# The last stage of a fused mixer and mixture-of-experts kernel: x1 held in SBUF, added by VectorE and GpSimd, and stored with plain DMAs

## The chip, the cores and the metric

The kernel runs on one core of a Trainium2 chip. The metric is the device time of one execution in microseconds, and lower is better. The kernel before has a median of 1121.13 us in three runs (1115.91 to 1122.24).

## The reference

x has the shape (4, 1024, 256), that is 4096 tokens of 256 values. Two residual blocks follow one another:

```python
x = x + _layernorm(_L0_attn_ref(_layernorm(x), ...))   # linear, conv, scan (cumprod, cumsum), gates
x = x + _layernorm(_L0_ffn_ref(_layernorm(x), ...))    # router, 8 experts with top 2, shared expert
```

The first line is called the mixer here, and its result is **x1**. In the second line each token goes to two of eight experts of 1024 hidden units (`silu(clip(gate)) * up @ down`) and to a shared expert of 256; the weighted sum of these is called **acc**. The output is `x1 + layernorm(acc)`, where the layer norm subtracts the mean of a token's 256 values and divides by the root of their variance plus 1e-5.

## The kernel before, in words

All tensors are fp32. Wherever a product must be exact, a value is split into a high part and a low part of type fp32r, and three matmuls stand for one.

**Mixer (to about 450 us).** Four batches of 1024 tokens are worked through in halves of 512, in an order that is written out by hand for every engine. x1 goes to the DRAM scratch `x1_scratch` (`store_x1`, L389, eight stores of 512 KB), the normalized tokens are scattered by expert to `xs_scratch` (L1232), and the shared expert's result goes to `acc_scratch`.

**Experts (about 450 to 1070 us).** `experts()` runs 39 slots. A slot is 256 tokens of one expert (8 steps), or 128 for the seven small slots n = 4, 8, ..., 28, whose weights have a ring of their own (`single_ring`, in the places of `xnt`, `w_sh`, `n2` and of `h`, `s`, `g`). On TensorE, slot follows slot without a gap. SyncE's queue (SP) loads weights and rows in `turn`; it waits there for TensorE (`down_done`) before it overwrites a chunk. `slots` unrolls the first slots, then runs a loop of four slots per pass, then unrolls slots 29 to 38. GpSimd adds each slot's result to `acc_scratch` with indirect accumulating DMAs (L1409). Beside this, SP moves x1 in `move_x1`, one chunk after each of the turns 2 to 8: the 4096 tokens are NC = 8 chunks of 512 tokens, four tiles of 128 x 256 each. The even chunks are copied from `x1_scratch` straight to the output in DRAM (L1376), the odd chunks are loaded to SBUF in the place of `e_both` (L1378).

**Last stage (from about 1070 us to the end).** After the last accumulating DMA, SP issues eight loads of acc (L1392, 512 KB each). Then four engines work on a chunk c in turn:

- VectorE, `moments_of(c)`: four `bn_stats` (L1673), four `bn_aggr` (L1678) and two small `tensor_scalar` (L1681, L1682). It signals `moments`.
- GpSimd, `root(c)`: a power of 128 x 4 (L1419) and a product (L1421). It signals `rs_ready`.
- ScalarE: four activations of 128 x 256 (L1590). They signal `normed`.
- The residual: for an odd chunk VectorE adds x1 in SBUF (`add_x1`, L1688, 128 x 1024) and SP stores the sum to the output (L1396); for an even chunk GpSimd issues an accumulating DMA (`add_out`, L1427) that adds acc to the x1 that already lies in the output.

Each engine goes through a fixed list. VectorE: moments 0 to 3, add 1, moments 4 and 5, add 3, moments 6 and 7, adds 5 and 7. GpSimd: roots 0 to 2, accumulating DMA 0, roots 3 and 4, DMA 2, roots 5 and 6, DMA 4, root 7, DMA 6. The program ends when SP has seen all stores of both kinds land (L1397, L1398).

Of the kernel before, what the change touches and what calls it, by code (L numbers as in the profile page):

```python
# [67 lines left out]
def mixer(nc, x, w_e, w_s, weights, full, consts, shared, xs_dram, x1_dram, acc_dram, fill, vec, ident,  # L68
# [3 lines left out]
    with ExitStack() as ctx:  # L72
# [124 lines left out]
        def free(engine, what):  # L197
# [36 lines left out]
        acc += [by_tile(flat(s[:, :, :]))]  # L234
        e_flat = e_both[:, :, :, :].rearrange("p h s c -> p (h s c)")
        x1 = [by_tile(e_flat[:, k * TC * D:(k + 1) * TC * D]) for k in range(4)]
        homes = (ring, low_d, [v[:, :, 0:W_ROW] for v in single_ring], quad(u_flat[:, R_AT:R_AT + 2 * GT * ROW]), quad(x_home[0]), quad(x_home[1]),
                 u_flat[:, R_AT + 2 * GT * ROW:R_AT + 2 * GT * ROW + DC * G].rearrange("p (c g) -> p c g", g=G),
                 cv_flat[:, 0:4 * G].rearrange("p (i g) -> p i g", g=G),
# [1012 lines left out]
TC = 4  # L1252
# [8 lines left out]
def experts(nc, ctx, w_s, xs_dram, acc_dram, x1_dram, out, group_expert, group_change, group_row, group_code, vec, ident, neg_half,  # L1261
# [24 lines left out]
    acc_loaded = [sem(f"f_loaded{c}") for c in range(NC)]  # L1286
    order, aggregated, moments = sem("f_order"), sem("f_aggregated"), sem("f_moments")
    rooted, rs_ready, normed = sem("f_rooted"), sem("f_rs_ready"), sem("f_normed")
    x1_moved, out_added = sem("x1_moved"), sem("out_added")
    sum_ready, sum_stored = sem("sum_ready"), sem("sum_stored")  # L1290

    gu_ps, down_ps = banks[0:2], [banks[2:4], banks[4:6]]
# [22 lines left out]
    def sync(sp):  # L1315
        def next_rows(i, n):
            to = (n + 1) % 2
            rows_of_slot, tiles = (P, 1) if single(n + 1) else (G, GT)
            row = sp.value_load(group_row[0:1, bass.ds(table_at(i, n + 1), 1)], min_val=0, max_val=SPARE)
            sp.wait_ge(x_turned, before(i, n, one) * DC + DC)  # L1320
            sp.wait_ge(meta_ready, before(i, n, one))
            sp.dma_start(rows[:, to, 0:tiles, :], xs_dram[bass.ds(row, rows_of_slot), :].rearrange("(t p) d -> p t d", p=P)
                         ).then_inc(rows_loaded[to], 16)

        def load_chunk(f, e, **cond):
            if f == FC - 2:
                sp.dma_start(low_d.bitcast(F32), w_s[e, f, :, 0:2 * D], **cond).then_inc(loaded[f], 16)
                sp.dma_start(ring[f][:, GU_HI:W_ROW].bitcast(F32), w_s[e, f, :, GU_HI:W_ROW], **cond).then_inc(loaded[f], 16)
                return
            sp.dma_start(ring[f].bitcast(F32), w_s[e, f, :, :], **cond).then_inc(loaded[f], 16)  # L1330

        def load_singles(part, e, wanted):
            first = sum(v.shape[1] for v in w_single[0:part])
            to = w_single[part].bitcast(F32)
            sp.dma_start(to, w_s[e, first:first + to.shape[1], :, :].rearrange("f p c -> p f c"), cond=wanted).then_inc(single_loaded, 16)

        def turn(i, n):
            if single(n):
                if n + 1 < SLOTS:
                    next_rows(i, n)  # L1340
                return
            e = sp.value_load(group_expert[0:1, bass.ds(table_at(i, n), 1)], min_val=0, max_val=E - 1)
            new = sp.value_load(group_change[0:1, bass.ds(table_at(i, n), 1)], min_val=0, max_val=1)
            last = n - 2 if single(n - 1) else n - 1
            to_come = NP + before(i, n, ones_at)
            loads_single = n % BODY in (2, 3) and single(n + BODY - n % BODY)
            for f in range(FC):
                sp.wait_ge(down_done, before(i, last, steps_at) + f + 1 + FC)
                if f == FC - 2 and single(n - 1):
                    next_rows(i, n)  # L1350
                load_chunk(f, e, cond=new)
                if f == 0 and not single(n - 1):
                    next_rows(i, n)
                if loads_single and f == 0:
                    e_single = sp.value_load(group_expert[0:1, bass.ds(to_come, 1)], min_val=0, max_val=E - 1)
                    flag = to_come + (0 if n % BODY == 2 else NS)
                    wanted = sp.value_load(group_change[0:1, bass.ds(flag, 1)], min_val=0, max_val=1)
                    if n > BODY:
                        sp.wait_ge(down_done, before(i, n - n % BODY, steps_at) + FC // 2 + FC)
                if loads_single and f < len(w_single):  # L1360
                    load_singles(f, e_single, wanted)

        def first_rows(b, par=0):
            row = sp.value_load(star[0:1, 1 + par:2 + par], min_val=0, max_val=SPARE)
            sp.dma_start(rows[:, par, :, :], xs_dram[bass.ds(row, G), :].rearrange("(t p) d -> p t d", p=P)
                         ).then_inc(rows_loaded[par], 16)

        def first_weights():
            e = sp.value_load(star[0:1, 0:1], min_val=0, max_val=E - 1)
            for f in range(FC):  # L1370
                load_chunk(f, e)

        def others():
            def move_x1(c):
                if c % 2 == 0:
                    sp.dma_start(token_rows(out)[c, :, :, :], token_rows(x1_dram)[c, :, :, :]).then_inc(x1_moved, 16)  # L1376
                else:
                    sp.dma_start(x1[c // 2], token_rows(x1_dram)[c, :, :, :]).then_inc(x1_moved, 16)  # L1378

            free(sp, "x1")  # L1380
            move_x1(0)
            free(sp, "tables")
            for c in range(1, NC):
                turn(0, c + 1)
                move_x1(c)
            slots(sp, turn, NC + 1)
            for par in range(2):
                sp.wait_ge(rows_loaded[par], 16 * before(0, SLOTS, same_at[par]))
            for par in range(2):
                sp.wait_ge(y_added[par], 16 * before(0, SLOTS, adds_at[par]))  # L1390
            for c in range(NC):
                sp.dma_start(acc[c], acc_dram[c * TC * P:(c + 1) * TC * P, :].rearrange("(t p) d -> p t d", p=P)  # L1392
                             ).then_inc(acc_loaded[c], 16)
            for c in range(1, NC, 2):
                sp.wait_ge(sum_ready, c // 2 + 1)
                sp.dma_start(token_rows(out)[c, :, :, :], acc[c]).then_inc(sum_stored, 16)  # L1396
            sp.wait_ge(sum_stored, 16 * (NC // 2))  # L1397
            sp.wait_ge(out_added, 16 * (NC // 2))  # L1398
        return first_rows, first_weights, lambda: next_rows(0, 1), others

    def gpsimd(pool):
# [11 lines left out]
        def rest():  # L1413
            free(pool, "acc")
            slots(pool, add_y)

            def root(c):
                pool.wait_ge(moments, c + 1)
                nc.gpsimd.tensor_tensor(rs[:, c, :], ve[:, c, :], neg_half[:, 0:TC], ALU.pow).then_inc(rooted, 1)  # L1419
                pool.wait_ge(rooted, c + 1)  # L1420
                nc.gpsimd.tensor_tensor(nm[:, c, :], mv[:, c, :, 0], rs[:, c, :], ALU.mult).then_inc(rs_ready, 1)  # L1421

            def add_out(c):
                if c == 0:
                    pool.wait_ge(x1_moved, 16 * NC)
                pool.wait_ge(normed, c + 1)
                nc.gpsimd.dma_start(token_rows(out)[c, :, :, :], acc[c], accum_op=ALU.add).then_inc(out_added, 16)  # L1427

            root(0)
            root(1)  # L1430
            for c in range(2, NC):
                root(c)
                if c % 2 == 0:
                    add_out(c - 2)
            add_out(NC - 2)
        return rest

    def tensor(pe):
# [103 lines left out]
    def scalar(act):  # L1542
# [39 lines left out]
        def rest():  # L1582
# [4 lines left out]
            for c in range(NC):  # L1587
                act.wait_ge(rs_ready, c + 1)
                for t in range(TC):
                    i = nc.scalar.activation(acc[c][:, t, :], acc[c][:, t, :], ACT.Identity, bias=nm[:, c, t:t + 1],  # L1590
                                             scale=rs[:, c, t:t + 1])
                i.then_inc(normed, 1)
        return first_hi, rest

    def vector(dve):
# [68 lines left out]
        def rest(plan_singles):  # L1664
# [5 lines left out]
            def moments_of(c):  # L1670
# [2 lines left out]
                    i = nc.vector.bn_stats(st[:, c, t, :], acc[c][:, t, :])  # L1673
                i.then_inc(order, 1)
                dve.wait_ge(order, c + 1)
                dve.sem_inc(seen, 1)
                for t in range(TC):
                    i = nc.vector.bn_aggr(mv[:, c, t, :], st[:, c, t, :])  # L1678
                i.then_inc(aggregated, 1)
# [2 lines left out]
                nc.vector.tensor_scalar(ve[:, c, :], mv[:, c, :, 1], 1.0, EPS, ALU.mult, ALU.add).then_inc(moments, 1)  # L1682

            def add_x1(c):
                if c == 1:
                    dve.wait_ge(x1_moved, 16 * NC)
                dve.wait_ge(normed, c + 1)
                nc.vector.tensor_tensor(acc[c], acc[c], x1[c // 2], ALU.add).then_inc(sum_ready, 1)  # L1688

            for c in range(NC):  # L1690
                moments_of(c)
                if c % 2 == 1 and c > 1:
                    add_x1(c - 2)
# [107 lines left out]
```

## Time and profile before

| | |
|---|---|
| median of three runs | 1121.13 us (1115.91 to 1122.24) |
| the profiled execution, its own time | 1116.39 us |
| its span | 1114.5 us |
| TensorE busy | 1022.9 us (92%) |
| VectorE, ScalarE, GpSimd busy | 801.9, 623.8, 286.8 us |
| mean granted TensorE clock | 0.978 |
| last expert result's DMA issued; first acc load issued | 1072.96 us; 1076.82 us |
| last instruction that computes ends; last store issued | 1105.7 us; 1105.73 us |
| DMA traffic | 210.30 MB, mean 189 GB/s |

Times inside the profile are microseconds from the start of the span. An instruction's row gives its start and its duration, and in brackets how long its engine was idle before it and what ended that. "To landing" is the time from the issue of a DMA to its completion. The profiled execution is at the low end of the three runs, 4.7 us below their median.

### The profile page before, as it was taken

How to read it: one execution, taken by the hardware profiler on the slowest of the kernel's cores; microseconds unless marked ns; L12 is line 12 of the kernel's file. 1: busy time of each engine (PE TensorE's matmuls, PEld its weight loads, DVE VectorE, ACT ScalarE, POOL GpSimd, SP SyncE). 2: the span in 40 equal slices, each digit the busy share in tenths (PEclk: the TensorE clock that was granted, in tenths of full speed). 3: DMA queues.
4: the chain of work that ended last, by engine and by line, in shares of the span. 5: the costliest groups of instructions: out<-in, count | busy, mean ns of one | idle time of the engine just before them, and what ended most of it. 6: DMA issues, size and time to landing. Idle time of an engine off the chain costs nothing.

```text
span 1114.5 us, 21512 instructions
## 1 busy us (share of the span) xinstructions
PE 1022.9 (92%) x7026; PEld 902.9 (81%) x7026; DVE 801.9 (72%) x2059; ACT 623.8 (56%) x1265; POOL 286.8 (26%) x303
## 2 busy tenths in 40 slices
PE   4889999989998999899999999999999999999930
PEld 2666677667676566799999999999999999999930
DVE  4997799888888857766666666666666666666645
ACT  6867868786876446344454444444544445445425
POOL 1133123453262273212121121211211212122134
PEclk9899999999999999999999999999999999999975
DMA  8656667886576588955563521735366822655149
GB/s 302 219 198 207 221 222 228 272 263 219 165 263 213 182 274 305 379 198 174 151 218 74 216 36 21 266 107 178 66 229 225 288 35 36 213 181 159 25 120 200
DMA packets 116518, 210.30 MB, mean 189 GB/s; under 512 B 9952, under 2 KB 75232, under 8 KB 116448
## 3 DMA queue, kind: packets, MB, share of 16 engines
q1 hardware_dynamic: 101040, 189.51, 49.0%
q0 software_dynamic: 15408, 19.93, 10.5%
q8 instruction: 35, 0.57, 0.2%
q14 instruction: 35, 0.29, 0.1%
HBM read 341.43 MB, written 86.02 MB: 384 GB/s over the span
## 4 chain that ended last, share of the span: by engine, by line
PE 75%; DVE 11%; DMA 4%; issue 3%; POOL 3%; ACT 2%; SPq 0%; DVEq 0%; ACTq 0%; POOLq 0%
PE bank L488 12%; PE bank L1461 10%; PE bank L1463 10%; PE bank L1462 10%; PE bank L1506 5%; PE bank L1508 5%; PE bank L1507 5%; PE bank L482 4%; PE bank L483 3%; PE bank L484 3%; POOL xs_scratch L1232 2%; DMA w_both<-w_split 1%; DVE h L925 1%; PE bank L1447 1%; PE bank L1479 1%
## 5 line engine op out<-in xcount | busy, mean ns | idle before, releaser
L1409 POOL DMA_INDIRECT acc_scratch<-cv,ids x71 | 111.5, 1571 | 504.1 <-DVE cv L1606 494.4
L1643 DVE TENSOR_SCALAR cv<-bank 128x256 f32<-128x256 f32 x284 | 120.5, 424 | 155.1 <-PE bank L1463 136.3
L1573 ACT ACTIVATE cv<-cv 128x256 f32<-128x256 f32 x284 | 118.4, 417 | 183.7 <-DVE cv L1643 183.7
L1461 PE MATMUL bank<-h_hi,w_both 128*128 128x256 f32 x640 | 178.0, 278 | 2.2 <-DMA w_both<-w_split 1.0
L1463 PE MATMUL bank<-h_hi,w_both 128*128 128x256 f32 x640 | 177.2, 277 | 0.0
L1462 PE MATMUL bank<-h_hi,w_both 128*128 128x256 f32 x640 | 177.2, 277 | 0.0
L1559 ACT ACTIVATE h_lo<-cv 128x256 fp32r<-128x256 f32 x256 | 106.8, 417 | 92.1 <-DVE cv L1646 92.1
L1646 DVE TENSOR_TENSOR cv<-bank,cv 128x256 f32<-128x256 f32 x284 | 120.3, 424 | 41.7 <-ACT cv L1573 34.6
L1461 PEld LDWEIGHTS bank<-h_hi,w_both 128*128 128x128 f32 x640 | 120.2, 188 | 3.1 <-issue 2.3
L1463 PEld LDWEIGHTS bank<-h_hi,w_both 128*128 128x128 f32 x640 | 120.3, 188 | 0.0
L1462 PEld LDWEIGHTS bank<-h_hi,w_both 128*128 128x128 f32 x640 | 120.3, 188 | 0.0
L482 PE MATMUL bank<-xs_hi,w_both 128*128 128x512 f32 x224 | 97.5, 435 | 20.7 <-DVE delta L875 9.7
L1624 DVE TENSOR_TENSOR w_both<-cv,h_lo 128x256 fp32r<-128x256 f32 x256 | 106.3, 415 | 0.5 <-ACT h_lo L1559 0.5
L484 PE MATMUL bank<-xs_hi,w_both 128*128 128x512 f32 x224 | 88.4, 395 | 0.0
L1508 PE MATMUL bank<-w_both 128*128 128x256 f32 x320 | 88.4, 276 | 0.0
L1506 PE MATMUL bank<-w_both,h_lo 128*128 128x256 f32 x320 | 88.4, 276 | 0.0
L1507 PE MATMUL bank<-w_both,h_lo 128*128 128x256 f32 x320 | 88.4, 276 | 0.0
L483 PE MATMUL bank<-xs_lo,w_both 128*128 128x512 f32 x224 | 88.1, 393 | 0.0
L1232 POOL DMA_INDIRECT xs_scratch<-n,slot_now x64 | 68.6, 1073 | 61.5 <-DVE slot_now L1013 32.5
L1215 POOL TENSOR_TENSOR h_lo<-h,h_hi 128x512 fp32r<-128x512 f32 x32 | 48.7, 1525 | 111.9 <-ACT h_hi L746 111.8
L482 PEld LDWEIGHTS bank<-xs_hi,w_both 128*128 128x128 f32 x224 | 42.6, 190 | 38.1 <-DVE delta L875 14.9
L1037 DVE TENSOR_TENSOR e_both<-e_both 128x768 f32<-128x768 f32 x64 | 65.0, 1018 | 9.8 <-ACT e_both L798 9.8
(293 smaller groups left out, 2819.1 us busy)
## 6 DMA issues: line engine op xcount, KB each, us to landing
w_both<-w_split SPq DMA_DIRECT2D x155, 776.0 KB
single_ring<-w_split SPq DMA_DIRECT2D x14, 3880.0 KB
w_split<-e_both SPq DMA_DIRECT2D x128, 256.0 KB, 4.0
e_both<-w_e SPq DMA_DIRECT2D x64, 384.0 KB, 3.5
h_lo<-w_split SPq DMA_DIRECT2D x31, 776.0 KB
xs_lo<-w_split SPq DMA_DIRECT2D x31, 776.0 KB
single_ring<-w_split SPq DMA_DIRECT2D x14, 1552.0 KB
w_split<-e_both SPq DMA_DIRECT2D x64, 264.0 KB, 3.7
```

Of the source, the lines that this page charges most:

```text
L482: nc.tensor.matmul(out, hi, x_hi, start=first, stop=False)
L483: nc.tensor.matmul(out, hi, x_lo, start=False, stop=False)
L484: return nc.tensor.matmul(out, lo, x_hi, start=False, stop=last)
L488: return nc.tensor.matmul(out, w, x, start=first, stop=last)
L1461: nc.tensor.matmul(out, gu_hi[f][:, cols], xg_hi[:, par, c, :], start=c == 0, stop=False)
L1462: nc.tensor.matmul(out, gu_hi[f][:, cols], xg_lo[:, par, c, :], start=False, stop=False)
L1463: k = nc.tensor.matmul(out, gu_lo[f][:, cols], xg_hi[:, par, c, :], start=False, stop=c == DC - 1)
L1506: nc.tensor.matmul(out, hg_hi[f % 4][:, toks], d_hi[f], start=f == 0, stop=False)
L1507: nc.tensor.matmul(out, hg_hi[f % 4][:, toks], d_lo[f], start=False, stop=False)
L1508: k = nc.tensor.matmul(out, hg_lo[f % 4][:, toks], d_hi[f], start=False, stop=f == FC - 1)
L1643: nc.vector.tensor_scalar(half, gate_ps, CLIP, -CLIP, ALU.min, ALU.max).then_inc(clipped, 1)
L1646: nc.vector.tensor_tensor(half, up_ps, half, ALU.mult).then_inc(h_ready, 1)
```

## The change

- `x1` has eight places in SBUF instead of four: the four in `e_both`, which held chunks 1, 3, 5 and 7, now hold chunks 0 to 3, and there are `g`, `w_sh` and the two halves of `n2` for chunks 4 to 7. These four lie in the ring of the small slots, so they are loaded after slot 30: one after each of the turns 31 to 34, the first behind a wait for `down_done`. Chunks 0 to 3 are loaded as before, and SP's unrolled part ends after turn 4 instead of 8. The four copies from DRAM to DRAM are gone.
- The accumulating DMAs are gone. GpSimd adds x1 to chunks 0, 2 and 5 with a `tensor_tensor` of 128 x 1024, VectorE adds it to chunks 1, 3, 4, 6 and 7, the last in two halves of 128 x 512.
- SP stores all chunks with plain DMAs in the order 0, 1, 2, 3, 4, 6, 7 (two halves), 5. ScalarE signals `normed` after half of chunk 7 as well.
- The lists are rearranged, and GpSimd waits for `x1_moved` ahead of root 0. A `sem_inc(seen, 1)` of VectorE is gone.

```diff
+POOL_ADDS, DVE_ADDS = (0, 2, 5), (1, 3, 4, 6, 7)
+PAST = LEAD + BODY * REPEATS + 1
...
+        n2_flat = n2[:, :, :, :].rearrange("p h t d -> p (h t d)")
+        x1 += [by_tile(flat(g[:, :, :])), by_tile(w_sh[:, 0:TC * D]), by_tile(n2_flat[:, 0:TC * D]), by_tile(n2_flat[:, TC * D:2 * TC * D])]
...
             def move_x1(c):
-                if c % 2 == 0:
-                    sp.dma_start(token_rows(out)[c, :, :, :], token_rows(x1_dram)[c, :, :, :]).then_inc(x1_moved, 16)
-                else:
-                    sp.dma_start(x1[c // 2], token_rows(x1_dram)[c, :, :, :]).then_inc(x1_moved, 16)
+                sp.dma_start(x1[c], token_rows(x1_dram)[c, :, :, :]).then_inc(x1_moved, 16)
+
+            def turn_and_move(i, n):
+                turn(i, n)
+                if n > PAST and NC // 2 + n - PAST - 1 < NC:
+                    if n == PAST + 1:
+                        sp.wait_ge(down_done, before(0, PAST, steps_at) + FC)
+                    move_x1(NC // 2 + n - PAST - 1)
...
-            for c in range(1, NC):
+            for c in range(1, NC // 2):
                 turn(0, c + 1)
                 move_x1(c)
-            slots(sp, turn, NC + 1)
+            slots(sp, turn_and_move, NC // 2 + 1)
...
-            for c in range(1, NC, 2):
-                sp.wait_ge(sum_ready, c // 2 + 1)
-                sp.dma_start(token_rows(out)[c, :, :, :], acc[c]).then_inc(sum_stored, 16)
+            for c in (0, 1, 2, 3, 4, 6, 7, 5):
+                if c in POOL_ADDS:
+                    sp.wait_ge(pool_sums, POOL_ADDS.index(c) + 1)
+                elif c < NC - 1:
+                    sp.wait_ge(sum_ready, DVE_ADDS.index(c) + 1)
+                for k, part in enumerate((slice(0, TC // 2), slice(TC // 2, TC)) if c == NC - 1 else (slice(0, TC),)):
+                    if c == NC - 1:
+                        sp.wait_ge(sum_ready, len(DVE_ADDS) + k)
+                    sp.dma_start(token_rows(out)[c][:, part, :], acc[c][:, part, :]).then_inc(sum_stored, 16)
...
-            def add_out(c):
-                if c == 0:
-                    pool.wait_ge(x1_moved, 16 * NC)
+            def add_x1(c):
                 pool.wait_ge(normed, c + 1)
-                nc.gpsimd.dma_start(token_rows(out)[c, :, :, :], acc[c], accum_op=ALU.add).then_inc(out_added, 16)
-
-            root(0)
-            root(1)
-            for c in range(2, NC):
+                nc.gpsimd.tensor_tensor(acc[c], acc[c], x1[c], ALU.add).then_inc(pool_sums, 1)
+
+            pool.wait_ge(x1_moved, 16 * NC)
+            for c in range(NC):
                 root(c)
-                if c % 2 == 0:
-                    add_out(c - 2)
-            add_out(NC - 2)
+                if c in (2, 4):
+                    add_x1(c - 2)
+            add_x1(5)
...
-                i.then_inc(normed, 1)
+                    if t == TC - 1 or (c == NC - 1 and t == TC // 2 - 1):
+                        i.then_inc(normed, 1)
...
             for c in range(NC):
                 moments_of(c)
-                if c % 2 == 1 and c > 1:
-                    add_x1(c - 2)
-            add_x1(NC - 1)
+                if c in (2, 4):
+                    add_x1(c - 1)
+            for c in (4, 6, 7):
+                add_x1(c)
```

The order on VectorE around the first add, in the last stage. `xr` is the small statistics tile, `xnt` holds chunks 0 to 4 of acc, `f_loaded3` says that chunk 3 has landed. Before:

```order
L1673 BN_STATS xr<-xnt 128x6 [waits f_loaded3]
L1673 BN_STATS xr<-xnt 128x6 x3
L1678 BN_AGGR xr<-xr 128x2 [waits f_order]
L1678 BN_AGGR xr<-xr 128x2 x3
L1681 TENSOR_SCALAR xr<-xr 128x4 [waits f_aggregated]
L1682 TENSOR_SCALAR xr<-xr 128x4
L1688 TENSOR_TENSOR xnt<-xnt,e_both 128x1024 [waits f_normed,x1_moved]
L1673 BN_STATS xr<-xnt 128x6 [waits f_loaded4]
```

And now:

```order
L1691 TENSOR_SCALAR xr<-xr 128x4 [waits f_aggregated]
L1692 TENSOR_SCALAR xr<-xr 128x4
L1699 TENSOR_TENSOR xnt<-xnt,e_both 128x1024 [waits f_normed,x1_moved]
L1684 BN_STATS xr<-xnt 128x6 [waits f_loaded3]
L1684 BN_STATS xr<-xnt 128x6 x3
L1688 BN_AGGR xr<-xr 128x2 [waits f_order]
```

The add of chunk 1 has moved from behind the moments of chunk 3 to ahead of them. In the same way add 3 now stands ahead of moments 5 and adds 4, 6 and 7 behind moments 7.

The order on GpSimd from the root of chunk 2 to that of chunk 4. Before:

```order
L1419 TENSOR_TENSOR xr<-xr,neg_half 128x4 [waits f_moments]
L1421 TENSOR_TENSOR xr<-xr 128x4 [waits f_rooted]
L1427 DMA out<-xnt 128x4x256 [waits f_normed,x1_moved]
L1419 TENSOR_TENSOR xr<-xr,neg_half 128x4 [waits f_moments]
L1421 TENSOR_TENSOR xr<-xr 128x4 [waits f_rooted]
```

And now:

```order
L1432 TENSOR_TENSOR xr<-xr,neg_half 128x4 [waits f_moments]
L1434 TENSOR_TENSOR xr<-xr 128x4 [waits f_rooted]
L1438 TENSOR_TENSOR xnt<-xnt,e_both 128x1024 [waits f_normed]
L1432 TENSOR_TENSOR xr<-xr,neg_half 128x4 [waits f_moments]
L1434 TENSOR_TENSOR xr<-xr 128x4 [waits f_rooted]
```

The first accumulating DMA has become an add of 128 x 1024 in the same place. The second stands behind root 4 in both, and the third (chunk 5) now stands behind root 7; there is no fourth.

## Rows read from the trace of the kernel before

**Rows 1.** Page of the profile, parts 1 and 2: busy time, and 40 slices

```profile
span 1114.5 us, 21512 instructions
PE 1022.9 (92%) x7026; PEld 902.9 (81%) x7026; DVE 801.9 (72%) x2059; ACT 623.8 (56%) x1265; POOL 286.8 (26%) x303
...
PE   4889999989998999899999999999999999999930
```

**Rows 2.** Waits of TensorE, 540 to 1070 us (line waited for: us, times, longest)

```profile
PE bank L1461 <- DMA w_both<-w_split: 1.0, 2, 0.6
PE bank L1506 <- DVE w_both L1624: 0.3, 1, 0.3
```

**Rows 3.** Timeline of the last stage: start us, duration us, engine, line

```profile
1072.96 1.55 POOL L1409 DMA_INDIRECT acc_scratch<-cv,ids  x1 [0.30 <-issue]
1076.82 2.77 SPq L1392 DMA_DIRECT2D xnt<-acc_scratch  x5
...
1084.44 6.29 ACT L1590 ACTIVATE xnt<-xnt,xr 128x256 f32<-128x256 f32 x12 [16.53 <-POOL xr L1421]
...
1085.04 1.40 DVE L1673 BATCH_NORM_STATS2 xr<-xnt 128x6 f32<-128x256 f32 x4
...
1087.15 1.40 DVE L1673 BATCH_NORM_STATS2 xr<-xnt 128x6 f32<-128x256 f32 x4
1087.33 1.01 POOL L1419 TENSOR_TENSOR xr<-xr,neg_half 128x4 f32<-128x4 f32 x1 [0.83 <-DVE xr L1682]
1088.41 0.20 POOL L1421 TENSOR_TENSOR xr<-xr 128x4 f32<-128x4 f32 x1
...
1089.26 1.22 DVE L1688 TENSOR_TENSOR xnt<-xnt,e_both 128x1024 f32<-128x1024 f32 x1
1089.85 1.57 POOL L1419 TENSOR_TENSOR xr<-xr,neg_half 128x4 f32<-128x4 f32 x1
...
1102.37 2.07 ACT L1590 ACTIVATE s<-s,xr 128x256 f32<-128x256 f32 x4 [0.96 <-POOL xr L1421]
1104.48 1.23 DVE L1688 TENSOR_TENSOR s<-s,e_both 128x1024 f32<-128x1024 f32 x1 [3.31 <-ACT s L1590]
1105.73 0.37 SPq L1396 DMA_DIRECT2D out<-s  x1
```

**Rows 4.** DMA issues of the last stage: queue, count, KB, us to landing

```profile
out<-xnt SPq DMA_DIRECT2D x2, 512.0 KB, 5.8
...
out<-x_in POOLq DMA_DIRECT2D x1, 512.0 KB, 8.2
out<-s SPq DMA_DIRECT2D x1, 512.0 KB, 6.2
```

**Rows 5.** Timeline of the mixer, GpSimd's 128 x 512 subtraction beside VectorE

```profile
156.55 3.24 POOL L1215 TENSOR_TENSOR h_lo<-h,h_hi 128x512 fp32r<-128x512 f32 x2 [5.15 <-ACT h_hi L746]
156.60 2.05 DVE L1037 TENSOR_TENSOR e_both<-e_both 128x768 f32<-128x768 f32 x1
...
250.50 2.12 POOL L1215 TENSOR_TENSOR h_lo<-h,h_hi 128x512 fp32r<-128x512 f32 x1 [1.83 <-ACT h_hi L746]
250.52 0.95 DVE L1037 TENSOR_TENSOR e_both<-e_both 128x768 f32<-128x768 f32 x1
...
382.95 0.20 POOL L1193 TENSOR_TENSOR nm<-mv,rs 128x4 f32<-128x4 f32 x1
383.10 2.50 POOL L1215 TENSOR_TENSOR h_lo<-h,h_hi 128x512 fp32r<-128x512 f32 x2
```

**Rows 6.** Source lines L1215 and L870: duration ns min/median/max

```profile
L1215 POOL TENSOR_TENSOR h_lo<-h,h_hi x32: 1266/1298/2190, 47.7 to 388.3; 128x512 fp32r<-128x512 f32 x32
...
L870 DVE TENSOR_TENSOR xs_lo<-cv,xs_hi x16: 680/683/740, 30.3 to 314.2; 128x512 fp32r<-128x512 f32 x16
```

**Rows 7.** Source line L389, the 512 KB stores of x1: landing times

```profile
DMA to landing us min/median/max: 3.6/4.8/6.9
```

**Rows 8.** DMA queues, 1080 to 1116 us: packets, MB, share of 16 engines

```profile
q1 hardware_dynamic: 5895, 5.84, 47.9%
q0 software_dynamic: 2112, 2.10, 44.5%
```

**Rows 9.** Windows: start:end, us, engines' busy us, PEclk, DMA share, GB/s

```profile
972.50:975.50 3.00, 3.00 (x29) 3.00 (x29) 2.45 (x9) 2.04 (x5) 0.00 (x0) 1.00 1.01 408
989.30:991.30 2.00, 2.00 (x20) 2.00 (x20) 1.50 (x6) 1.60 (x5) 0.00 (x0) 1.00 0.00 0
991.30:1010.00 18.70, 18.30 (x161) 18.11 (x160) 12.25 (x34) 8.75 (x22) 3.17 (x2) 1.00 0.95 338
```

**Rows 10.** Timeline of TensorE, the wait between 990 and 1030 us

```profile
1006.28 0.38 PE L1461 MATMUL bank<-h_hi,w_both 128*128 128x256 f32 x1 [0.40 <-DMA w_both<-w_split]
```

More of the change, by code:

```diff
@@ L1288, in experts @@
     rooted, rs_ready, normed = sem("f_rooted"), sem("f_rs_ready"), sem("f_normed")
-    x1_moved, out_added = sem("x1_moved"), sem("out_added")
+    x1_moved, pool_sums = sem("x1_moved"), sem("pool_sums")
     sum_ready, sum_stored = sem("sum_ready"), sem("sum_stored")
@@ L1393, in others @@
                              ).then_inc(acc_loaded[c], 16)
-            for c in range(1, NC, 2):
-                sp.wait_ge(sum_ready, c // 2 + 1)
-                sp.dma_start(token_rows(out)[c, :, :, :], acc[c]).then_inc(sum_stored, 16)
-            sp.wait_ge(sum_stored, 16 * (NC // 2))
-            sp.wait_ge(out_added, 16 * (NC // 2))
+            for c in (0, 1, 2, 3, 4, 6, 7, 5):
[7 more added lines that the diff above has]
+                    sp.dma_start(token_rows(out)[c][:, part, :], acc[c][:, part, :]).then_inc(sum_stored, 16)
+            sp.wait_ge(sum_stored, 16 * (NC + 1))
         return first_rows, first_weights, lambda: next_rows(0, 1), others
@@ L1675, in moments_of @@
                 dve.wait_ge(order, c + 1)
-                dve.sem_inc(seen, 1)
                 for t in range(TC):
@@ L1684, in add_x1 @@
             def add_x1(c):
-                if c == 1:
+                if c == DVE_ADDS[0]:
                     dve.wait_ge(x1_moved, 16 * NC)
-                dve.wait_ge(normed, c + 1)
-                nc.vector.tensor_tensor(acc[c], acc[c], x1[c // 2], ALU.add).then_inc(sum_ready, 1)
+                for k, part in enumerate((slice(0, TC // 2), slice(TC // 2, TC)) if c == NC - 1 else (slice(0, TC),)):
+                    dve.wait_ge(normed, c + 1 + k)
+                    nc.vector.tensor_tensor(acc[c][:, part, :], acc[c][:, part, :], x1[c][:, part, :], ALU.add).then_inc(sum_ready, 1)
             for c in range(NC):
                 moments_of(c)
-                if c % 2 == 1 and c > 1:
-                    add_x1(c - 2)
-            add_x1(NC - 1)
+                if c in (2, 4):
+                    add_x1(c - 1)
+            for c in (4, 6, 7):
+                add_x1(c)
         return seeds, first_lo, rest
```

## The prediction

> **What bounds the kernel now.** I read the page first: TensorE is busy for 1022.9 of 1114.5 us, and its slices stay at eight or nine tenths up to the last two [rows 1]. Then the waits of TensorE among the expert slots: 1.3 us in 530 us [rows 2]. So a change outside TensorE's work can move the time in two ways: it makes TensorE wait, or it changes the stage after the last slot. That stage runs from the last accumulating DMA at 1072.96 to the last store, issued at 1105.73 [rows 3] and landed 6.2 us later, at 1111.9 [rows 4]; 2.6 us of closing work complete the span. Nothing on TensorE covers this stage, so a microsecond here is a microsecond of the kernel. The timeline shows what paces it. VectorE's moments of two chunks stand 2.11 us apart (1085.04, 1087.15) without waits for data, and behind the last moments come root, four activations (2.07 us), one add (1.23) and one store, each released by the one before [rows 3].
>
> **What the change does outside the last stage: nothing, I take.** Four copies inside DRAM leave the early slots and four loads of 512 KB join slots 31 to 34. SP issues them behind the last chunk of each turn; the added wait of turn 31 asks for the downs of slot 30, which the turn's own last wait has already seen, so it holds nothing up. Two of the four places matter. At 972.5 the DMA engines are full (share 1.01) with an expert's weights; the load goes behind them and nothing behind it is urgent for several us. At 989.3 they are idle for 2 us, then comes an expert's load at share 0.95, inside which TensorE waits 0.40 us for a chunk [rows 9, 10]. The new load takes 0.5 MB / 408 GB/s = 1.3 us, about the idle gap in front. Bounds: 0 if it fits the gap, +1.3 us if it pushes that chunk. I take 0. TensorE did not wait beside the old copies either, so their removal gives 0 (bounds 0 and -0.3, the part of rows 2 that could be theirs). The missing `sem_inc` and SP's shorter unrolled part (it waits for TensorE before each chunk anyway) go together at 0.
>
> **The last stage, durations.** VectorE's add: 1.22 us [rows 3]; its half: 0.68 [rows 6]. GpSimd's add of 128 x 1024 does not exist before. A 128 x 4 takes 0.20 [rows 3], a 128 x 512 takes 1.30 at the median [rows 6], so 1.1 us per 508 columns and **2.4 us** for 1024; ends 2.3 and 2 x 1.52 = 3.0 (1.52 being 48.7 us / 32, L1215 with its collisions). I take 2.4.
>
> **The two engines exclude each other.** This carries the forecast. Where GpSimd's 128 x 512 started at 156.55 and VectorE's two-input operation at 156.60, the latter took 2.05 us instead of 0.95: it stood still until 157.70, that is 1.15 us after GpSimd's start. At 250.50 against 250.52 VectorE won, and GpSimd took 2.12 instead of 1.30 [rows 5]. In the last stage GpSimd's power of 1.01 takes 1.57 behind an add of VectorE [rows 3]. The change puts three long GpSimd adds where VectorE wants to add as well.
>
> **Who starts first.** Root 2 ends at 1088.61. A GpSimd operation that is ready is recorded 0.05 us before the end of the one ahead (383.10 against 382.95 + 0.20) [rows 5], so add 0 starts at 1088.56. VectorE's add 1 needs the eighth activation, which ends at 1084.44 + 8 x 0.52 = 1088.60, and starts 0.04 later as at 1104.48, so at 1088.64. GpSimd is 0.08 us ahead: by rows 5 enough (0.05 was, 0.02 was not). The second pair (add 2 behind root 4, add 3 behind the activations of chunk 3) meets the same way: root 4 follows root 3 by one set of moments (2.11), the activations follow root 3 by 0.03 + 2.07 + 0.04, and GpSimd is about 0.07 ahead.
>
> **The sum, step by step** (before in brackets):
> - Moments 2 leave VectorE at 1087.15. It now waits 1.5 us for add 1, then until GpSimd has let go at 1088.56 + 2.25 = 1090.8, and ends at about 1092.1. Moments 3 start at 1092.0 (1087.15); moments 4 are ready at 1096.3 (1092.6), 3.7 late, since add 1 stood between 3 and 4 already.
> - Root 3 ends at 1095.6, activations 3 at 1097.7. VectorE is free from 1096.2, and add 3 asks at 1097.75. GpSimd's add 2 has the port until 1100.0; add 3 ends at 1101.2 (1095.8), 5.4 late.
> - Moments 5, 6, 7 follow without adds between; moments 7 are ready at 1107.5 (1100.05), 7.5 late. That is 5.4 plus one set of moments (2.11), since moments 5 stood ahead of add 3 before.
> - Root 7 waits behind add 4 of VectorE (1107.4 to 1108.6, as the 1.57 row) and ends at 1109.8. Activations 7 run to 1111.9, half of them to 1110.9 (1104.44).
> - GpSimd's add 5 starts behind VectorE's add 6, at 1110.05, and holds VectorE's half 7a until 1112.3. 7a ends at 1113.0, 7b at **1113.6** (1105.7).
> - SP issues store 7b at 1113.63 and store 5, last in its list, at 1114.0.
> - Landing of store 5. Before, plain stores took 5.8 and 6.2 us beside accumulating DMAs [rows 4]; those moved 2.10 MB in 44.5% of 36 us, 131 GB/s, against 339 GB/s on the other queue (5.84 MB, 47.9%) [rows 8]. With them gone the nearest rows are the mixer's 512 KB stores, 3.6 at least, 4.8 at the median, 6.9 at most [rows 7]. I take 3.6 and 0.5 for the two halves just in front: 4.1, so 1118.1 (1111.9). The ends 3.6 and 6.9 go to the range.
>
> Sum: 1118.1 - 1111.9 = **+6.2 us**, span 1120.7. Of it +7.9 is compute that ends later, +0.4 the second store behind 7b, -2.1 the faster landing. Against the profiled execution (1116.39) that is 1122.6; on the median of 1121.13, 4.7 above it, **1127.3 us**.
>
> The Trainium skill (DMA: Bandwidth & Descriptors, section Anatomy of one DMA) gives a transfer about 2.0 us fixed plus its bytes at 436 GB/s, by which 512 KB would land in an estimated 3.2 us and the sum would be +5.3. No 512 KB row of rows 4 and 7 is that short.
>
> **Rivals.**
> - *R1, VectorE gets the port at both meetings.* The lead of 0.08 and 0.07 us lies between a case won (0.05) and one lost (0.02), and starts vary by as much from run to run. Then add 1 runs 1088.64 to 1089.9, GpSimd's add 0 to 1092.2 beside moments 3, which have one input, and add 3 ends at 1097.0. Each meeting gives 2.0 us back: 7b ends at 1109.6, store 5 lands at 1114.1, **+2.2 us**, not slower by 0.5%. One of two won: +4.2. It decides the sign of the verdict, its place is the two meetings, its price 2.0 us each. The Trainium skill (SBUF: State Buffer, section SBUF: two separate sides) says that whichever of the two starts first gets the pair for the whole instruction. By that GpSimd wins both; the row at 250.50 speaks against it at 0.02 us.
> - *R2, the stores were the limit, and the adds do not exclude each other at this size.* For it: the accumulating DMAs' 44.5%. Against it: rows 5. If the long adds block nothing, 7b still ends at 1108.2, 2.5 later than before, since VectorE idles 1.5 us ahead of each of adds 1 and 3 for the activations; store 5 goes out at 1108.6 and lands after 4.1: 1112.7, **+0.8 us**.
> - *R3, the load at 989.3 delays the weights.* TensorE waits up to 1.3 us more at 1006: **+7.5 us**. For it: 0.40 us of wait in a full stretch. Against it: 2 us of idle engines just ahead.
>
> **How the numbers follow.** Three runs of before spread over 6.3 us, so two medians of this kernel tell a difference only above about 0.5%, 5.6 us; the bound lies just under my sum. Chances: forecast 0.55, R1 with its half case 0.25, R2 0.12, R3 0.08. The forecast case runs from +5 (landing 3.6, add 2.3) to +10 (add 2.8, landing 6.2) before noise; with a median's noise of some 2 us three in five of it are beyond 5.6. Slower: 0.55 x 0.62 + 0.25 x 0.1 + 0.08 x 0.8 = 0.43; faster 0.06 (half of R2, by noise); within, the remaining 0.51. Range: R2's low end and noise, 1119.5, to the forecast's high end, 1131. The likeliest case alone: 1125 to 1131.
>
> **What would show it.** Right: GpSimd's first and second long adds at about 2.4 us and VectorE's adds 1 and 3 beside them at 3.3 to 3.5 instead of 1.22; moments 3 starting near 1092; the last store issued near 1114 and landing in about 4; TensorE's waits as before. Wrong: adds 1 and 3 at 1.22 with GpSimd's at 3.5 (R1); both undisturbed (R2); a TensorE wait above 1 us near 1006 (R3); or a last store that still needs 6 us with no accumulating DMA near it, which would undo the landing's 2.1.

## The result, and the profile after

The changed kernel takes 1122.31 us at the median (1120.42 to 1126.76, 20 runs), the kernel before 1118.77 us in the 20 runs beside it. The ratio is **1.003, 95% interval 1.002 to 1.0039**: slower by 2.2 to 4.4 us, where +6.2 was forecast. The direction held, and the stated range held the time, but the forecast change was nearly twice the measured one.

The first two lines of the page of the changed kernel answer to [rows 1]:

```profile
span 1121.4 us, 21553 instructions
...
PE 1028.7 (92%) x7026; PEld 906.8 (81%) x7026; DVE 807.8 (72%) x2061; ACT 623.8 (56%) x1265; POOL 289.2 (26%) x302
```

This profiled execution took 1123.61 us. The two profiled executions differ by 4.5 us before the last stage begins. 2.7 of these lie before 948 us, where the other eleven profiled kernels of this document differ from the kernel before by -0.6 to +4.5 us: one profile cannot tell this from scatter. The rest lies in the last expert slots and is taken up under loads_late. So the last stage is compared by itself from here on: **from the issue of the first acc load to the end of the span**. It took 1114.5 - 1076.8 = 37.7 us before and 1121.4 - 1081.3 = 40.1 us now, **+2.4 us**.

The timeline of the changed kernel's last stage, with the columns of [rows 3]:

```profile
1081.32 2.92 SPq L1400 DMA_DIRECT2D xnt<-acc_scratch  x5
...
1087.44 1.40 DVE L1684 BATCH_NORM_STATS2 xr<-xnt 128x6 f32<-128x256 f32 x4
...
1089.43 1.40 DVE L1684 BATCH_NORM_STATS2 xr<-xnt 128x6 f32<-128x256 f32 x4
...
1092.84 2.34 POOL L1438 TENSOR_TENSOR xnt<-xnt,e_both 128x1024 f32<-128x1024 f32 x1
1093.19 3.08 DVE L1699 TENSOR_TENSOR xnt<-xnt,e_both 128x1024 f32<-128x1024 f32 x1 [1.67 <-ACT xnt L1600]
...
1101.58 2.35 POOL L1438 TENSOR_TENSOR xnt<-xnt,e_both 128x1024 f32<-128x1024 f32 x1
1101.78 3.22 DVE L1699 TENSOR_TENSOR xnt<-xnt,e_both 128x1024 f32<-128x1024 f32 x1 [1.52 <-ACT xnt L1600]
...
1110.90 1.22 DVE L1699 TENSOR_TENSOR xnt<-xnt,g 128x1024 f32<-128x1024 f32 x1
1111.08 1.91 POOL L1432 TENSOR_TENSOR xr<-xr,neg_half 128x4 f32<-128x4 f32 x1 [0.71 <-DVE xr L1692]
...
1113.75 2.34 POOL L1438 TENSOR_TENSOR x_in<-x_in,w_sh 128x1024 f32<-128x1024 f32 x1
...
1114.95 2.29 DVE L1699 TENSOR_TENSOR s<-s,n 128x512 f32<-128x512 f32 x2 [1.22 <-ACT s L1600]
...
1117.68 0.50 SPq L1410 DMA_DIRECT2D out<-x_in  x1
```

The reader sees both meetings: GpSimd's add of 2.34 us starts 0.35 and 0.20 us ahead of VectorE's, and VectorE's adds take 3.08 and 3.22 us instead of 1.22. Ahead of each VectorE has been idle for 1.67 and 1.52 us. The third meeting is the planned one: VectorE's half 7a stands still until GpSimd's add 5 is through at 1116.09, and the two halves take 2.29 us together. The sets of moments stand 1.99 us apart (1087.44, 1089.43) where it was 2.11. The last add ends 35.9 us after the first acc load was issued (28.9 before), so the computing became 7.0 us longer.

What gives 4.6 of these back (7.0 - 2.4) stands in two views. First the DMA issues of the changed kernel's last stage, with the columns of [rows 4]:

```profile
out<-xnt SPq DMA_DIRECT2D x5, 512.0 KB, 3.0
...
out<-x_in SPq DMA_DIRECT2D x2, 512.0 KB, 3.1
...
out<-s SPq DMA_DIRECT2D x2, 256.0 KB, 2.3
```

A plain store of 512 KB lands in about 3 us now, against 5.5 to 6.2 before (two of the lines stand in [rows 4], with 5.8 and 6.2); the last takes 3.3 instead of 6.2. Second, the closing instructions. Source line L72 of the kernel before (duration ns min/median/max, first and last start):

```profile
L72 POOLq DRAIN  x1: 11666/11666/11666, 1102.3 to 1102.3; - x1
...
L72 SPq COMPARE_BRANCH  x1: 38/38/38, 1111.9 to 1111.9; - x1
```

and line L74 of the changed kernel:

```profile
L74 POOLq DRAIN  x1: 6862/6862/6862, 1113.0 to 1113.0; - x1
...
L74 SPq COMPARE_BRANCH  x1: 38/38/38, 1121.0 to 1121.0; - x1
```

SP is through with the last store at 1111.9 and 1121.0. Before, GpSimd's drain went on until 1114.0 and everything waited for it; now it ends at 1119.9 and nobody does. From SP's last wait to the end of the span it was 2.6 us and is 0.4. Landing gives 2.9 us back and the closing 2.2; 0.4 goes to the second store behind the last add.

### The profile page after: what moved, and what is told of

Same layout as the page of the kernel before. It is cut to its first block, busy times and chain, and to the rows that moved or that the text cites. A ratio compares the mean times of both kernels' runs of the same rounds, so it can differ in the third digit from the quotient of the medians.

```text
span 1121.4 us, 21553 instructions
## 1 busy us (share of the span) xinstructions
PE 1028.7 (92%) x7026; PEld 906.8 (81%) x7026; DVE 807.8 (72%) x2061; ACT 623.8 (56%) x1265; POOL 289.2 (26%) x302
## 4 chain that ended last, share of the span: by engine, by line
PE 77%; DVE 9%; DMA 5%; issue 3%; ACT 3%; POOL 3%; SPq 1%; DVEq 0%; POOLq 0%; ACTq 0%
PE bank L492 13%; PE bank L1471 10%; PE bank L1473 10%; PE bank L1472 10%; PE bank L1516 5%; PE bank L1518 5%; PE bank L1517 5%; PE bank L486 4%; PE bank L487 4%; PE bank L488 4%; DMA w_both<-w_split 1%; PE bank L1457 1%; PE bank L1489 1%; PE bank L1487 1%; PE bank L1488 1%
## 5 line engine op out<-in xcount | busy, mean ns | idle before, releaser
L1657 DVE TENSOR_TENSOR cv<-bank,cv 128x256 f32<-128x256 f32 x284 | 120.3, 423 | 41.8 <-ACT cv L1583 35.2
```

Of the source, the lines that this page charges most:

```text
L1657: nc.vector.tensor_tensor(half, up_ps, half, ALU.mult).then_inc(h_ready, 1)
```

## The experiments

The stage is measured in each run as above, in one profile per kernel. Its length scatters little: 40.1 and 40.0 us in the changed kernel and in loads_late, which have the same stage, and 34.9 and 34.8, 33.3 and 33.4 in two more such pairs. The ratios rest on 9 to 12 runs of a kernel, that of gp_store5 on 4 and that of all_vector_late on 6.

| run | stage, us | ratio to before, 95% interval |
|---|---|---|
| before | 37.7 | 1 |
| changed | 40.1 | 1.003 (1.002 to 1.0039) |
| no_read | 35.2 | 0.9993 (0.9973 to 1.0012) |
| vector_first | 36.9 | 0.9985 (0.9969 to 1.0001) |
| order_alone | 40.3 | 1.0024 (1.0002 to 1.0046) |
| seen_back | 40.8 | 1.0048 (1.0029 to 1.0067) |
| gp_store5 | 42.9 | 1.0056 (1.0034 to 1.0078) |
| gp_store0 | 38.7 | 1.0022 (1.0007 to 1.0037) |
| loads_late | 40.0 | 1.0021 (1.0006 to 1.0036) |
| all_vector | 33.3 | 0.9982 (0.9968 to 0.9996) |
| apart | 34.9 | 0.9985 (0.9969 to 1.0) |
| apart_late | 34.8 | 0.997 (0.9955 to 0.9985) |
| all_vector_late | 33.4 | 0.9949 (0.9929 to 0.9968) |

**no_read: GpSimd nearly as busy as in the changed kernel, but reading nothing.** Edit to the changed kernel:

```diff
-                nc.gpsimd.tensor_tensor(acc[c], acc[c], x1[c], ALU.add).then_inc(pool_sums, 1)
+                nc.gpsimd.memset(x1[c], 0.0).then_inc(wiped, 1)
+                pool.wait_ge(wiped, POOL_ADDS.index(c) + 1)
+                nc.gpsimd.memset(x1[c], 0.0).then_inc(pool_sums, 1)
```

> The changed kernel, but GpSimd writes constants twice over its x1 tile (about 2.1 us, no SBUF input) where it added x1; chunks 0, 2 and 5 leave out x1. The measure is the last stage, from the issue of the first acc load to the end of the span: 37.7 us before, 40.1 us with the change. Theory (the two engines exclude each other while both read SBUF): VectorE's adds 1 and 3 take 1.22 us instead of 3.08 and 3.22, the first half of add 7 takes 0.68 instead of 1.68, and the stage falls by 3.9 + 1.0, less up to 0.4 for what follows it, to 35.2 to 35.6 us. Rival (GpSimd being occupied for 2.3 us is what delays the roots and so everything): the stage stays at 39.5 to 40.1 us, and adds 1 and 3 still stand still.

Chunks 0, 2 and 5 come out without x1 here. Measured: 35.2 us. Timeline of no_read at the first meeting and at add 7:

```profile
1091.28 0.95 POOL L1438 MEMSET e_both<- 128x1024 f32 x1
1091.65 1.23 DVE L1701 TENSOR_TENSOR xnt<-xnt,e_both 128x1024 f32<-128x1024 f32 x1 [1.66 <-ACT xnt L1602]
1092.29 0.95 POOL L1440 MEMSET e_both<- 128x1024 f32 x1
...
1109.34 0.95 POOL L1440 MEMSET w_sh<- 128x1024 f32 x1
1109.56 0.69 DVE L1701 TENSOR_TENSOR s<-s,n 128x512 f32<-128x512 f32 x1 [1.22 <-ACT s L1602]
```

VectorE's adds run at 1.23 and 0.69 us in the middle of GpSimd's fills. So GpSimd's occupancy is not the cause: two fills keep it busy for 1.96 us where the add took 2.34. What differs is that the add reads two inputs from SBUF and the fill none; whether the reading or something else in the add blocks VectorE, this run does not separate. Without the blocking the stage is 40.1 - 35.2 = 4.9 us shorter, within the expected range.

**vector_first: the same adds, the other one first.**

```diff
             def add_x1(c):
+                if c != 5:
+                    nc.gpsimd.memset(rows[:, 0, :, :], 0.0)
                 pool.wait_ge(normed, c + 1)
```

> The changed kernel with a 0.54 us constant fill on GpSimd ahead of its adds 0 and 2, so that it comes second to both meetings. Theory (who starts first holds the other up for its whole length): VectorE's adds 1 and 3 take 1.22 us, GpSimd's adds 0 and 2 take 3.2 to 3.5 us instead of 2.34, the stage falls from 40.1 to 36.2 to 36.6 us although GpSimd has more to do. Rival (GpSimd's occupancy): the stage grows by up to 1.1 us, to 40.1 to 41.2 us.

Measured: 36.9 us, 3.2 us less by giving GpSimd 1.1 us *more* to do. VectorE's adds 1 and 3 take 1.23 us, GpSimd's adds 3.30 and 3.17. Timeline of vector_first:

```profile
1092.57 0.53 POOL L1438 MEMSET u<- 128x520 f32 x1
1092.94 1.23 DVE L1701 TENSOR_TENSOR xnt<-xnt,e_both 128x1024 f32<-128x1024 f32 x1 [1.66 <-ACT xnt L1602]
1093.07 3.30 POOL L1440 TENSOR_TENSOR xnt<-xnt,e_both 128x1024 f32<-128x1024 f32 x1
1094.08 1.40 DVE L1686 BATCH_NORM_STATS2 xr<-xnt 128x6 f32<-128x256 f32 x4
...
1095.93 0.47 DVE L1693 TENSOR_SCALAR xr<-xr 128x4 f32<-128x4 f32 x1
```

This is rival R1 made to happen. It gives back 3.2 us where R1 was priced at 2 x 2.0, and misses the expected 36.2 to 36.6 us by 0.3 to 0.7. Part of what is missing stands in the last row: a `tensor_scalar` with a single input takes 0.47 instead of 0.17 while GpSimd's add ends. The run apart shows it in full.

**order_alone: only VectorE's new order, in the kernel before.**

```diff
-                if c % 2 == 1 and c > 1:
-                    add_x1(c - 2)
+                if c in (2, 4):
+                    add_x1(c - 1)
+                if c == NC - 1:
+                    add_x1(5)
             add_x1(NC - 1)
```

> The kernel before with one part of the change: VectorE's add 1 stands ahead of moments 3 and add 3 ahead of moments 5; accumulating DMAs and all else as before. Theory (each of these adds waits 1.5 us for the activations, and nothing gives that back): idle 1.5 us ahead of each, last add ends 3.0 us later after the first acc load, stage 37.7 + 3.0 = 40.7 us. Rival (the order costs nothing, since GpSimd and ScalarE had slack): stage 37.7 us.

Measured: 40.3 us, +2.6. Adds 1 and 3 are preceded by 1.47 and 1.44 us of idle time, and the last add ends 32.0 us after the first load's issue (28.9 before), +3.1; landing was 5.6 instead of 6.2 for the last store, which accounts for the rest. The order alone costs as much as the whole change does in the end (+2.6 and +2.4 us in the stage).

**seen_back: the semaphore increment between the statistics.**

```diff
                 dve.wait_ge(order, c + 1)
+                dve.sem_inc(seen, 1)
                 for t in range(TC):
                     i = nc.vector.bn_aggr(mv[:, c, t, :], st[:, c, t, :])
```

> The changed kernel with the semaphore increment put back between VectorE's two statistics operations. Theory (the removed increment is why moments of two chunks now stand 2.00 us apart instead of 2.11): 2.11 us apart again, the stage 0.6 to 0.9 us longer, 40.7 to 41.0 us. Rival (the spacing has another cause, such as fewer DMAs beside it): 2.00 us apart and 40.1 us.

Measured: 40.8 us, +0.7; roots 1 and 2, which follow the moments, stand 2.12 us apart (1089.67, 1091.79), where the changed kernel has 2.00 (1089.60, 1091.60). So 0.7 us of gain came from a line that was costed at nothing. It stood in the list of VectorE, which paces this stage, eight times.

**gp_store5 and gp_store0: one plain store issued by GpSimd, the last or the first.**

```diff
+            pool.wait_ge(pool_sums, 3)
+            nc.gpsimd.dma_start(token_rows(out)[5, :, :, :], acc[5]).then_inc(pool_stored, 16)
```

In gp_store5 this stands behind GpSimd's add of chunk 5; in gp_store0 the same lines for chunk 0, with `pool_sums` at 1, stand behind root 3. SP leaves that store out.

> The changed kernel, but the store of chunk 5 is issued by GpSimd behind its own add, a plain store without adding. Theory (the closing drain of GpSimd waits for its own DMAs and ends about 2 us after they have landed, which the change has removed): GpSimd's drain ends 1.5 to 2.5 us after the last landing, the time from the last landing to the end of the span is 2 to 2.8 us as before instead of 0.4, the stage 40.1 to 42 us (the store goes out about 1 us earlier than in SP's list, and GpSimd takes 1.3 us to issue it). Rival (the 2.2 us were due to the adding in the DMAs, or to chance): closing 0.4 us and the stage at 38.5 to 40.1 us.

> The changed kernel, but the store of chunk 0, the first, is issued by GpSimd behind root 3. Theory: its DMA has landed and been accounted for long before the end, so the closing stays at 0.4 us; root 4 is ready by moments 4 at 2 us behind, so the 1.35 us of issue delay it by up to 0.4 us; the stage 40.1 to 40.8 us. Rival (any DMA of GpSimd in the last stage makes the drain slow): closing 2.6 us, stage 42.3 us or more.

Measured: gp_store5 42.9 us, gp_store0 38.7 us. Closing lines of gp_store5, source line L74:

```profile
L74 POOLq DRAIN  x1: 7525/7525/7525, 1117.7 to 1117.7; - x1
...
L74 SPq COMPARE_BRANCH  x1: 38/38/38, 1122.4 to 1122.4; - x1
```

GpSimd's store went out at 1117.8 and landed in 4.2 us, at 1122.0; the drain ended at 1125.2, 3.2 us after that, and the span 0.6 us later. In the kernel before, its last accumulating DMA landed at 1110.6 (1102.36 + 8.2) and the drain ended 3.4 us later, at 1114.0. So the adding is not needed for it: a late plain store of GpSimd's kept its drain open about as long beyond the landing. The closing came out at 3.4 us, above the 2 to 2.8 expected, the drain ended 3.2 us behind the landing where 1.5 to 2.5 were expected, and the stage of 42.9 us is above the 40.1 to 42: this landing was itself nearly the last, 0.4 us ahead of the end of SP's wait. order_alone, which keeps the accumulating DMAs, gives the same distance once more: landing 7.6 us after 1107.27, drain ended at 1118.3, 3.4 us later. In gp_store0 the closing is about 0.7 us (SP's last wait ends at 1118.1, the span at 1118.8): an early DMA does not matter.

The drain is not free without a late DMA either. In the changed kernel GpSimd's last add ends at 1116.1 and the drain at 1119.9, 3.8 us later, and this distance is 3.8 to 3.9 in the ten profiled kernels in which GpSimd issues no DMA near the end. It stays hidden only because the last store has not landed by then: 1.1 us are left in the changed kernel.

The 38.7 us of gp_store0 missed its expectation, 40.1 to 40.8, on the good side. Issuing the store delayed root 4, and so GpSimd's add 2, past the start of VectorE's add 3. Timeline of gp_store0:

```profile
1100.53 1.23 DVE L1703 TENSOR_TENSOR xnt<-xnt,e_both 128x1024 f32<-128x1024 f32 x1 [1.25 <-ACT xnt L1604]
1100.63 3.33 POOL L1439 TENSOR_TENSOR xnt<-xnt,e_both 128x1024 f32<-128x1024 f32 x1
```

At 0.10 us apart VectorE went first, and the meeting turned around by itself. One meeting turned gave 1.4 us here, two in vector_first gave 3.2.

**loads_late: x1 of chunks 4 to 7 loaded behind the last turn.**

```diff
-            slots(sp, turn_and_move, NC // 2 + 1)
+            slots(sp, turn, NC // 2 + 1)
+            for c in range(NC // 2, NC):
+                move_x1(c)
```

> The changed kernel, but x1 of chunks 4 to 7 is loaded behind the last turn, in SP's 20 us of waiting, instead of among turns 31 to 34. Theory (those loads cost TensorE nothing): the time is that of the changed kernel within 1 us (ratio to before 1.002 to 1.004), TensorE's waits from 900 us on the same within 0.3 us. Rival (the loads delay an expert's weights or rows by up to 1.3 us): the time falls by 1 us or more, and TensorE's waits for w_both and h_lo shrink from 1.5 us in all.

Measured: stage 40.0, ratio 1.0021 against 1.003, intervals overlapping; the difference, 1.0 us, lies just where theory and rival meet. TensorE's waits from 900 us on, in the changed kernel (columns as in [rows 2]):

```profile
PE bank L1471 <- DMA w_both<-w_split: 0.7, 1, 0.7
PE bank L1516 <- DVE w_both L1635: 0.3, 1, 0.3
PE bank L1471 <- DMA h_lo<-w_split: 0.2, 1, 0.2
```

and in loads_late:

```profile
PE bank L1473 <- DMA w_both<-w_split: 0.7, 1, 0.7
PE bank L1518 <- DVE w_both L1637: 0.3, 1, 0.3
```

A wait of 0.2 to 0.8 us for the chunk in `h_lo` is there in six of the eight profiled kernels that load x1 among the turns, and in none of the five that do not (before, order_alone and the three late ones). In the changed kernel it falls at 979.65, in an expert's load that starts right behind the x1 load of 958.5.

The traces show more than these waits. GpSimd issues 71 accumulating DMAs of expert results in every kernel. From the 55th to the last of them the changed kernel takes 129.8 us, the kernel before 128.1 (to 1072.96, [rows 3]). Timeline of the changed kernel:

```profile
947.53 1.56 POOL L1422 DMA_INDIRECT acc_scratch<-cv,ids  x1 [0.30 <-issue]
...
1077.33 1.56 POOL L1422 DMA_INDIRECT acc_scratch<-cv,ids  x1 [0.30 <-issue]
```

and of the kernel before:

```profile
944.86 1.55 POOL L1409 DMA_INDIRECT acc_scratch<-cv,ids  x1 [0.30 <-issue]
```

loads_late takes 128.7 us for this stretch, 1.1 less than the changed kernel. The eight kernels that load x1 among the turns take 129.4 to 130.4 us, 129.8 in the mean; the five others take 128.1 to 129.4, 128.7 in the mean. So the loads among the turns cost about 1.1 us, with one profile per kernel behind it.

**all_vector, apart, and both with late loads.** The lists, in the notation m (moments), a (VectorE's add), r (root), p (GpSimd's add):

```diff
-DVE   m0 m1 m2 a1 m3 m4 a3 m5 m6 m7 a4 a6 a7     GpSimd r0 r1 r2 p0 r3 r4 p2 r5 r6 r7 p5
+DVE   m0 m1 m2 a0 m3 a1 m4 a2 m5 m6 a3 m7 a4 a5 a6 a7     GpSimd r0 to r7     (all_vector)
+DVE   m0 m1 m2 m3 a1 m4 m5 m6 a3 m7 a4 a5 a6 a7     GpSimd r0 r1 p0 r2 r3 r4 p2 r5 r6 r7     (apart)
```

> The changed kernel with all eight adds on VectorE and none on GpSimd: add 0 behind moments 2, adds 1, 2 behind moments 3 and 4, add 3 behind moments 6, adds 4 to 7 behind moments 7; all stores by SP in the order of chunks. Theory (worked out with 2.00 us per set of moments, 1.14 per add, 2.05 per chunk on ScalarE, 1.4 us per store): no add blocked, the last add ends 30.4 us after the first acc load is issued, the stage is 34 us (before 37.7, changed 40.1), ratio to before 0.996 to 0.998. Rival (VectorE becomes the bound, with 25 us of its own work, and eats the gain): 36 to 38 us.

Measured: stage 33.3 us (34 expected), ratio 0.9982 (0.996 to 0.998 expected). The exclusion works the other way round as well: the power in a root behind an add of VectorE takes 1.91 us here instead of 1.01. No add is blocked, and the last ends 29.9 us after the first load's issue. SP stores its last half directly behind it. The profile alone would promise 4.4 us against before; the whole time gained 0.4 to 3.6.

> The changed kernel with the lists set so that no add of GpSimd meets one of VectorE: GpSimd adds 0 (behind root 1) and 2 (behind root 4) while VectorE works on moments, which have one input; VectorE adds 1 (behind moments 3), 3 (behind moments 6) and 4 to 7 (behind moments 7); stores in the order of chunks. Theory (only the meetings cost, GpSimd's help is worth its adds): all of GpSimd's adds 2.34 us, all of VectorE's 1.22, last add about 2.3 us earlier than with all adds on VectorE, stage 30.8 to 31.5 us against 33.3, ratio to before 0.995 to 0.997. Rival (GpSimd's adds push the roots late and ScalarE then sets the pace): stage 33 us or more.

Measured: stage 34.9 us where 30.8 to 31.5 were expected, on the rival's side: worse than with GpSimd left out. The adds themselves are undisturbed, as expected (2.35 and 1.22 us). The cost is elsewhere. Timeline of apart:

```profile
1087.81 2.35 POOL L1438 TENSOR_TENSOR xnt<-xnt,e_both 128x1024 f32<-128x1024 f32 x1 [0.30 <-ACT xnt L1599]
1087.90 2.28 DVE L1690 TENSOR_SCALAR xr<-xr 128x4 f32<-128x4 f32 x1
...
1096.69 2.35 POOL L1438 TENSOR_TENSOR xnt<-xnt,e_both 128x1024 f32<-128x1024 f32 x1
...
1097.12 1.94 DVE L1690 TENSOR_SCALAR xr<-xr 128x4 f32<-128x4 f32 x1
```

The small `tensor_scalar` that negates four means takes 2.28 and 1.94 us instead of 0.17. It has one input, but it did not run beside GpSimd's add. The statistics (`bn_stats`, `bn_aggr`) did, in vector_first. Each set of moments ends with such an operation, and both adds of GpSimd in this run stop VectorE for about 2 us, to save it one add of 1.14 each. Where GpSimd's add started just behind one of VectorE, as in vector_first, the same operation lost only 0.3 us. The assumption in apart's expectation that moments are safe was wrong, and so was the rival's reason: roots and ScalarE were late because VectorE was.

> The kernel of the run apart, with x1 of chunks 4 to 7 loaded behind the last turn as in loads_late. Theory (the loads among turns 31 to 34 cost TensorE 0.2 to 0.8 us of waiting for h_lo): no wait for h_lo on TensorE from 900 us on, the same stage as apart, ratio 0.0002 to 0.001 lower. Rival (the loads cost nothing, the waits shift by chance): the same ratio.

> All eight adds on VectorE and x1 of chunks 4 to 7 loaded behind the last turn. Theory: stage 33.3 us as in all_vector, no wait for h_lo on TensorE from 900 us on, ratio 0.0002 to 0.001 below the 0.9982 of all_vector. Rival (all of the head is as before or the loads cost nothing): 0.9982.

Measured: apart_late 34.8 us and 0.997 (apart 0.9985); all_vector_late 33.4 us and 0.9949 (all_vector 0.9982). The wait for `h_lo` is gone in both, the stages are unchanged. Together with loads_late (0.0009 lower) all three pairs point the same way, by 0.0009, 0.0015 and 0.0033, or 1 to 3.7 us. 0.0002 to 0.001 was expected of the last two, so both gained more. The stretch of the last slots (see loads_late) is shorter by 1.5 us in apart_late than in apart (128.2 and 129.7) and by 1.1 in all_vector_late than in all_vector (129.0 and 130.1), that is 0.001. Moving the loads helps by about that; where the rest of the 3.7 us of all_vector_late comes from, if it is not scatter between runs, stays open.

**all_vector_late beats both kernels**: 1114.39 us at the median of 6 runs, ratio to before 0.9949 (0.9929 to 0.9968). The lists of apart and all_vector change nothing in what is computed.

## Why the prediction was right or wrong

The direction and the mechanism were right, the size was not: +6.2 was forecast, +2.4 is what the stage shows and +3.5 the medians. The likeliest case had its own range of 1125 to 1131; the median is below it. Of the 5.0 us between the forecast of 1127.3 and 1122.31, 2.4 are the starting point: the median of before was 1121.13 in three runs and 1118.77 in twenty. **The step that failed most is the closing work, put down as a fixed 2.6 us;** it measured 0.4. Step by step:

- **Bound.** Right. TensorE's work was untouched and the stage decided most of it.
- **Outside the stage, 0.** Low by about 1 us. By the medians the part outside the stage is 3.5 - 2.4 = +1.1 us, with an interval as wide as itself, and the stretch of the last slots gives the same 1.1 over thirteen traces. This is within the bounds of 0 and 1.3. The one new wait that the changed kernel's trace shows, 0.2 us at 979.65, is at another load (958.5) than the two that were looked at.
- **GpSimd's add, 2.4.** Measured 2.34.
- **Exclusion, and who starts first.** Right at all three places. GpSimd's lead was 0.35 and 0.20 us, not 0.08 and 0.07. It would have won without the closer moments too: with them set back to 2.12 us apart its leads were 0.15 and 0.09 (seen_back). At every meeting in the last stage the engine whose recorded start was earlier went at full speed and the other waited, down to 0.09 us for GpSimd (seen_back) and 0.10 for VectorE (gp_store0).
- **Add 1 ends 15.3 us after the first load's issue, add 3 after 24.4, moments 7 after 30.7, last add after 36.8.** Measured 15.0, 23.7, 29.7, 35.9. Most of the 0.9 is the spacing of the moments. What failed here is "the missing `sem_inc` ... at 0": it was worth 0.7 us by seen_back, whose last add ends after 36.6.
- **Landing, 4.1.** Measured 3.3. The end of the range at 3.6 was already too long: without accumulating DMAs beside them, 512 KB stores land in 3.0 at the median here. The trace is near the 3.2 that the prediction worked out from the Trainium skill (DMA: Bandwidth & Descriptors, section Anatomy of one DMA), and the sum by it, +5.3, was the better one. But the Trainium skill gives that fit for DMAs issued by GpSimd, and these stores are SP's; the two plain stores that GpSimd issued landed in 3.5 and 4.2 us (gp_store0, gp_store5).
- **"2.6 us of closing work complete the span", taken as fixed.** This is the step that failed, and the largest error. It was no fixed cost: it was GpSimd's drain, which ended 3.4 us behind the landing of its last accumulating DMA, and the change removed that DMA; gp_store5 brought a closing of 3.4 us back with one late DMA. 2.2 us of gain were missed, because the prediction rested on no closing row; the drain of 11.7 us stands in the trace of before.

Together: 6.2 - 0.9 - 0.8 - 2.2 = 2.3, against 2.4 measured in the stage. With about 1.1 us in the last slots that makes the 3.5 of the medians.

The rivals: R1 did not occur in the changed kernel; forced, it gave back 3.2 of the 4.0 us that it was priced at. R2 is out: adds 1 and 3 took 3.08 and 3.22 us beside GpSimd's adds, and 1.23 beside its fills in no_read. R3's size of up to 1.3 us was near the 1.1 found in the last slots, though the wait in the changed kernel's trace is not at the load that it named. R2's sense that the stores mattered was half right: landing (6.2 to 3.3) and drain (2.6 to 0.4) together gave some 5 us, and the computing took 7.0.

## What to carry to other kernels

Before work is moved from VectorE to GpSimd, list what VectorE runs beside it: here a GpSimd add of 2.34 us stopped a VectorE add and even a 128 x 4 `tensor_scalar` until it had finished, so that handing over two adds of 1.14 us made the stage 1.6 us longer (apart against all_vector). Do not place an operation on the pacing engine ahead of independent work that is ready: two adds moved one step forward waited 1.47 and 1.44 us (order_alone). And when a change removes the last DMA of a queue, look at the drain that closes the program, which may end microseconds after the last data has landed.

## What the runs showed of the hardware that was not expected

- GpSimd's drain ended 3.2 to 3.4 us after the landing of its last DMA where that DMA was late (gp_store5, before, order_alone), plain or accumulating, and 3.8 to 3.9 us after its last operation where there was none or an early one; only the first kind delayed the end.
- A one-input fp32 `tensor_scalar` of 128 x 4 in SBUF took 2.28 and 1.94 us beside a GpSimd add (0.17 alone), while `bn_stats` in vector_first kept its 1.40 us for four beside one. Constant fills of GpSimd (0.95 us for 128 x 1024) disturbed neither an add of VectorE (1.23) nor `bn_stats` (1.40 for four); no `tensor_scalar` ran beside one.
- One semaphore increment between two VectorE operations cost about 0.1 us each time: sets of moments 2.12 us apart with it, 2.00 without.
- With four accumulating DMAs of 512 KB in the stage plain stores landed in 5.5 to 6.2 us; without them in 3.0 at the median. No run has as many plain stores on GpSimd's queue, so the adding and the second queue are not told apart.
